# First stage of an LRU-convolution plus LoRA MLP kernel: weight loads, tap tables, the first tile's x and its A product in another order

## The reference, cut to what matters

```python
# x: (64, 32, 512) = batch, head, length
x = x + conv(x, itok_B_8_3872, ...)      # part one, per head h:
#   K[h, l] = 2 Re sum_n Cs[h, n] exp(dtA[h, n] l)      (taps, 64 complex modes)
#   y = causal convolution of x * mask with K[h] + D[h] * x, times mask
x = x + mlp(x, ..., itok_B_2_6, 0)       # part two, per batch row b with its LoRA index:
#   gate = x Wg^T + (x Ag^T) Bg^T / 2 ;  up = x Wu^T + (x Au^T) Bu^T / 2
#   act = silu(gate) * up                (1376 columns)
#   down = act Wd^T + (act Ad^T) Bd^T / 2
```

## Time and profile before

| what | value |
|---|---|
| median of three runs | 562.81 us (562.47 to 563.48) |
| the profiled execution's own time | 563.44 us |
| its span in the trace | 561.6 us |
| granted TensorE clock, mean of the span | 0.993 |
| TensorE busy | 520.0 us, 93% of the span |
| VectorE, ScalarE, GpSimd busy | 46%, 36%, 7% |
| chain of work that ended last | TensorE 86%, VectorE 5%, DMA 5%, SP queue 2% |

### The profile page before, as it was taken

How to read it: one execution, slowest core, us unless ns; L and a number is a source line. 1 busy time by engine, 2 the same in 40 slices (tenths; PEclk the granted TensorE clock), 3 DMA queues, 4 the chain that set the end, 5 groups by cost and what they waited for, 6 DMA issues and landing times.

```text
span 561.6 us, 10112 instructions
## 1 busy us (share of the span) xinstructions
PE 520.0 (93%) x3169; PEld 474.1 (84%) x3169; DVE 258.5 (46%) x556; ACT 199.8 (36%) x426; POOL 39.9 (7%) x55
## 2 busy tenths in 40 slices
PE   0087899999999999999999999999999999999997
PEld 0086787889899998989898989898989898999986
DVE  7855265844343535353535353444444443525341
ACT  4863006534333423232423332333334333324321
POOL 1006600100000000000000000000000000000000
PEclk9998899999999999999999999999999999999999
DMA  7898993304040403040303121121304040404000
GB/s 281 326 299 294 309 350 81 88 6 118 1 118 6 112 11 110 13 110 13 100 22 91 32 81 42 55 68 32 91 13 109 0 123 0 116 7 110 13 20 19
DMA packets 32306, 53.19 MB, mean 95 GB/s; under 512 B 7586, under 2 KB 16194, under 8 KB 32290
## 3 DMA queue, kind: packets, MB, share of 16 engines
q1 hardware_dynamic: 32290, 53.00, 31.7%
HBM read 48.69 MB, written 4.28 MB: 94 GB/s over the span
## 4 chain that ended last, share of the span: by engine, by line
PE 86%; DVE 5%; DMA 5%; SPq 2%; issue 1%; ACT 1%; DVEq 0%
PE ps_u L940 21%; PE ps_g L940 21%; PE ps_db L978 13%; PE ps_da L978 13%; PE ps_x L969 3%; DMA kpad<-k_sb 3%; PE ps_g L892 2%; PE ps_x L919 2%; DMA toep<-kpad 2%; PE ps_u L892 2%; PE ps_g L950 2%; PE ps_g L951 2%; PE ps_u L950 2%; PE ps_u L951 2%; PE ps_x L1011 1%; DVE wd_lo L729 1%
## 5 line engine op out<-in xcount | busy, mean ns | idle before, releaser
L469 ACT CAST b_spl<-b_raw 64x512 fp32r<-64x512 f32 (+1 forms) x96 | 54.5, 571 | 97.1 <-PE ps_u L951 79.1
L766 DVE TENSOR_TENSOR b_spl<-b_raw,b_spl 64x512 fp32r<-64x512 f32 (+1 forms) x96 | 60.7, 633 | 57.0 <-ACT b_spl L469 53.3
L940 PE MATMUL ps_g<-w_hi,x_hi 128*128 128x512 f32 (+1 forms) x192 | 72.7, 379 | 0.2 <-DVE x_lo L759 0.2
L940 PE MATMUL ps_u<-w_hi,x_hi 128*128 128x512 f32 (+1 forms) x192 | 71.3, 371 | 0.0
L940 PE MATMUL ps_u<-w_lo,x_hi 128*128 128x512 f32 (+1 forms) x192 | 71.3, 371 | 0.0
L940 PE MATMUL ps_u<-w_hi,x_lo 128*128 128x512 f32 (+1 forms) x192 | 71.3, 371 | 0.0
L940 PE MATMUL ps_g<-w_lo,x_hi 128*128 128x512 f32 (+1 forms) x192 | 71.1, 370 | 0.0
L940 PE MATMUL ps_g<-w_hi,x_lo 128*128 128x512 f32 (+1 forms) x192 | 71.0, 370 | 0.0
L978 PE MATMUL ps_da<-wd_hi,ht_hi 128*128 128x288 f32 (+1 forms) x176 | 54.6, 310 | 1.4 <-DVE wd_lo L729 1.4
L802 DVE TENSOR_TENSOR h_act<-h_act,ps_u 128x512 f32<-128x512 f32 (+1 forms) x48 | 30.4, 633 | 54.1 <-PE ps_u L951 54.0
L978 PE MATMUL ps_db<-wd_hi,ht_hi 128*128 128x288 f32 (+1 forms) x176 | 53.3, 303 | 0.0
(11 more groups left out here) (165 smaller groups left out, 920.8 us busy)
## 6 DMA issues: line engine op xcount, KB each, us to landing
a_raw<-atab SPq DMA_DIRECT2D x64, 152.0 KB, 2.5
toep<-kpad SPq DMA_DIRECT2D x16, 512.0 KB, 6.3
b_raw<-btab SPq DMA_DIRECT2D x128, 64.0 KB, 2.1
um<-xr SPq DMA_DIRECT2D x16, 256.0 KB, 4.4
x<-xT SPq DMA_DIRECT2D x8, 512.0 KB, 8.4
w_raw<-wgu SPq DMA_DIRECT2D x8, 512.0 KB, 9.1
out<-y_sb SPq DMA_DIRECT2D x15, 256.0 KB, 2.1
b_raw<-btab SPq DMA_DIRECT2D x64, 44.0 KB, 1.8
```

The source lines that it names most:

```text
L469: nc.scalar.copy(b_spl[0:LR, up, 0:w], b_raw[slot][:, up * w:(up + 1) * w]).then_inc(b_hi, 1)
L766: V.tensor_tensor(b_spl[LR:P, up, 0:w], b_raw[slot][:, up * w:(up + 1) * w], b_spl[0:LR, up, 0:w].bitcast(F32), ALU.subtract).then_inc(b_l ...
L940: T.matmul(ps[:, 0:w], xs[:, q, kb, :], ws[:, kb, col:col + w], start=(kb == 0 and xs is x_hi and ws is w_hi), stop=False)
```

## The change

On the SP queue, weight pieces 8 and 9 leave their place ahead of the first store of taps; all of pieces 8 to 11 stand behind Toeplitz loads 0 to 3. The first half of x of group 2 no longer stands ahead of the store of group 1: the four half-groups of x of groups 2 and 3 follow one by one behind the Toeplitz loads of pairs 4 to 7. The stores of group 2 and 3 stand behind the Toeplitz loads of pairs 6 and 7 instead of behind those of pairs 7 and 8. On VectorE `phases(3)` comes before `taps(1)`; `add_conv(0)` ahead of `tables(2)`, and `tables(3)` ahead of `taps(2)`; TensorE does `taps(2)` after conv 2 and `taps(3)` after conv 3.

For the first tile, x is split in two steps: the high and low parts of heads 0 to 27 are made while convs 14 and 15 run; pair 15's result is written first for the four batch rows of the tile, then x of heads 28 to 31 is copied, then the rest of the result is written, and the small high and low parts follow. TensorE's `lora_a(0)` stands behind `base(0, 0)`. In the first tile ScalarE's splits of the down weights start ahead of `silu(0)`, each two pieces one step earlier than before, and VectorE's `rem_part`s likewise.

```diff
@@ SP queue
-            load_piece(2 * KB)
-            load_piece(2 * KB + 1)
             sp.wait_ge(idx_in, 16)
             ids0 = indices(0, 0)
             sp.wait_ge(zero_out, 16)
             store_taps(0)
             for pair in range(RC):
-                load_toep(pair, pair, 0, True)
-            load_piece(2 * KB + 2)
-            load_piece(2 * KB + 3)
-            load_x(2, 0)
+                load_toep(pair, pair, 0)
+            for n in range(2 * KB, NP_GU):
+                load_piece(n)
             store_taps(1)
-            load_x(2, 1)
             for pair in range(RC, 2 * RC):
                 load_um(pair, pair - RC, False)
-                load_toep(pair, pair - RC, 1, False)
-                if pair < RC + 2:
-                    load_x(3, pair - RC)
-            store_taps(2)
+                load_toep(pair, pair - RC, 1)
+                if pair >= RC + 2:
+                    store_taps(pair - RC)
+                load_x(2 + (pair - RC) // 2, pair % 2)
...
                 if pair == 2 * RC:
-                    store_taps(3)
                     load_a(0, 0, ids0)
@@ ScalarE, first tile
+                if first:
+                    top_part(NP_GU)
+                    top_part(NP_GU + 1)
                 silu(0)
                 b_hi_part(a, q, 1, 0)
                 b_hi_part(a, q, 1, 1)
                 if first:
-                    top_part(NP_GU)
-                    top_part(NP_GU + 1)
+                    top_part(NP_GU + 2)
+                    top_part(NP_GU + 3)
...
-            x_hi_part(0, 0, True)
+            act.wait_ge(xt_ok, 1)
+            nc.scalar.copy(x_hi[:, 0, :, 0:(NH - 4) * BT], xt[:, :, 0:(NH - 4) * BT]).then_inc(x0_hi, 1)
+            act.wait_ge(xt_ok, 2)
+            nc.scalar.copy(x_hi[:, 0, :, (NH - 4) * BT:P], xt[:, :, (NH - 4) * BT:P]).then_inc(xhi_ok, 1)
@@ VectorE
+            def select_conv(pair, b0, b1):
+                dve.wait_ge(conv_ps, pair + 1)
+                dve.wait_ge(x_in[2 * pair // HG], 32)
+                return V.copy_predicated(
+                    x[:, 2 * pair:2 * pair + 2, :, b0:b1],
+                    lmask[:, :, b0:b1].unsqueeze(1).broadcast_to([P, 2, KB, b1 - b0]),
+                    ps_c[pair % RC][:, :].rearrange("p (h k b) -> p h k b", h=2, k=KB)[:, :, :, b0:b1])
...
             tables(1)
+            phases(3)
             taps(1)
-            phases(3)
-            tables(2)
-            taps(2)
...
             add_conv(0)
+            tables(2)
             tables(3)
+            taps(2)
+            add_conv(1)
             taps(3)
-            for pair in range(1, PAIRS - 2):
+            for pair in range(2, PAIRS - 2):
...
             take_x(0, NH - 4).then_inc(xt_ok, 1)
             add_conv(PAIRS - 2)
-            add_conv(PAIRS - 1)
-            dve.wait_ge(x1_ok, PAIRS)
+            dve.wait_ge(x0_hi, 1)
+            first_x_lo(0, NH - 4).then_inc(x0_lo, 1)
+            select_conv(PAIRS - 1, 0, BT).then_inc(x0_sel, 1)
+            dve.wait_ge(x1_ok, PAIRS - 1)
+            dve.wait_ge(x0_sel, 1)
             take_x(NH - 4, NH).then_inc(xt_ok, 1)
-            x_lo_part(0, 0, True)
+            select_conv(PAIRS - 1, BT, NB).then_inc(x1_ok, 1)
+            dve.wait_ge(xhi_ok, 1)
+            first_x_lo(NH - 4, NH).then_inc(xlo_ok, 1)
@@ TensorE
             conv(1)
             conv(2)
+            taps(2)
             conv(3)
-            taps(2)
-            conv(4)
             taps(3)
...
-                if first:
-                    lora_a(t)
...
                 if first:
+                    lora_a(t)
                     base(0, 1)
                     lora(0, 0)
```

More of the change, by code:

```diff
@@ L163, in program @@
         conv_ps, x1_ok = sem("conv_ps"), sem("x1_ok")
+        x0_hi, x0_lo, x0_sel = sem("x0_hi"), sem("x0_lo"), sem("x0_sel")
         a_in = sem("a_in")
@@ L217, in program, with taps_rows, shifted_taps @@
         DT, NAR, DAR, DAI = 8, 9, 10, 11
+        def taps_rows(g):
+            return bass.AP(tensor=kpad, offset=g * HG * (P + NL) + P, ap=[[PB, PA], [P + NL, HG], [1, PB]])
+        def shifted_taps(pair):
+            return bass.AP(tensor=kpad, offset=pair * (2 * (P + NL)) + 1, ap=[[1, P], [P + NL, 2], [1, NL]])
         block = top.enter_context(nc.Block())
@@ L235, in store_taps, with load_toep @@
                 sp.wait_ge(k_ready, g + 1)
-                dst = bass.AP(tensor=kpad, offset=g * HG * (P + NL) + P, ap=[[PB, PA], [P + NL, HG], [1, PB]])
-                sp.dma_start(dst, k_sb[:, g, :, :]).then_inc(k_out[g], 16)
-            def load_toep(pair, slot, group, first):
+                sp.dma_start(taps_rows(g), k_sb[:, g, :, :]).then_inc(k_out[g], 16)
+            def load_toep(pair, slot, group):
                 sp.wait_ge(k_out[group], 16)
[L242 to L245, removed]
+                wait(sp, conv_ps, pair - RC + 1)
+                sp.dma_start(toep[:, slot, :, :], shifted_taps(pair)).then_inc(toep_in[slot], 16)
             def load_um(pair, slot, first):
@@ L317, in _ @@
                 load_um(pair, pair % RC, False)
-                load_toep(pair, pair % RC, pair // RC, False)
+                load_toep(pair, pair % RC, pair // RC)
                 if pair == 2 * RC:
-                    store_taps(3)
                     load_a(0, 0, ids0)
@@ L525, in body @@
                 if first:
-                    top_part(NP_GU + 2)
-                    top_part(NP_GU + 3)
-                ht_hi_part(0)
-                if first:
                     top_part(NP_GU + 4)
                     top_part(NP_GU + 5)
+                ht_hi_part(0)
                 silu(2)
@@ L819, in body @@
                 V.tensor_tensor(cols(wd_lo), ad, cols(wd_hi).bitcast(F32), ALU.subtract).then_inc(ad_lo, 1)
+                if first:
+                    rem_part(NP_GU)
+                    rem_part(NP_GU + 1)
                 b_lo_part(a, q, 1, 0)
@@ L828, in body @@
                 if first:
-                    rem_part(NP_GU)
-                    rem_part(NP_GU + 1)
+                    rem_part(NP_GU + 2)
+                    rem_part(NP_GU + 3)
                 b_lo_part(a, q, 2, 0)
@@ L834, in body @@
                 if first:
[L835 to L838, removed]
                     rem_part(NP_GU + 4)
                     rem_part(NP_GU + 5)
+                ht_lo_part(0)
                 if not last:
@@ L857, in _, with first_x_lo @@
             b_lo_part(0, 0, 0, 1)
+            def first_x_lo(h0, h1):
+                cols = slice(h0 * BT, h1 * BT)
+                return V.tensor_tensor(x_lo[:, 0, :, cols], xt[:, :, cols], x_hi[:, 0, :, cols].bitcast(F32),
+                                       ALU.subtract)
             dve.wait_ge(x1_ok, PAIRS - 2)
@@ L904, in _ @@
             conv(2)
+            taps(2)
             conv(3)
-            taps(2)
-            conv(4)
             taps(3)
-            for pair in range(RC + 1, PAIRS):
+            for pair in range(RC, PAIRS):
                 conv(pair)
@@ L934, in base @@
                     if c == 0 and not up:
+                        if first:
+                            pe.wait_ge(x0_lo, 1)
                         pe.wait_ge(xlo_ok, t + 1)
```

## The result

The changed kernel takes 559.44 us (median of 5 executions, 558.71 to 560.04) against 562.47 us of the kernel before (5 executions, 562.13 to 563.48): a ratio of 0.9943, 95% interval 0.9929 to 0.9957. It is 3.0 us faster where 1.95 were predicted; the span of the profiled execution goes from 561.6 to 557.6 us.

The account below looks back on a forecast made before the run. The first 106 us, a chain of waits through DMA stores, x preparation and tile 0, were taken as the bound. -2.5 - 1.05 + 1.6 = -1.95 us from 562.81 gave 560.8 us; forecast 559.5 to 561.7, range with rivals 558.2 to 563.2.

Parts of the forecast that it names:

- Stretch 1: From the start to the landing of pair 9's Toeplitz matrix: 2.5 us earlier, with ends of 0.4 and 4.
- The main term: Group 2's store no longer empties the DMA queue at 50 to 58 us: 3.4 us gained.
- The gain at the first store: Without pieces 8 and 9 ahead, group 0's store lands at 24.8 instead of 25.73: gain 0.95 (0 to 0.95).
- the first part: Within the first stage: 0.95 us gained at group 0's store, 1.8 lost to pieces 8 and 9 behind Toeplitz loads.
- The order of the tables: VectorE's new order ahead of the taps costs nothing, covered by 4 us or more of queued traffic.
- Stretch 2: From conv 15's end to the first base product: 2.50 us becomes about 1.45, gain 1.05 (0.5 to 1.1).
- Stretch 3: Tile 0, first base product to down product: 20.5 us becomes about 22.05, loss 1.6 (0.9 to 2.5).
- Both waits: TensorE's new waits in tile 0: 1.05 us for the low part of B, about 1.1 at the x transposes.
- The queue gives more: Rival: pieces fill holes, pair 9 lands 4 us earlier, TensorE's lower clock mostly avoided; about 558.5 us, chance 0.17.
- The queue gives nothing: Rival: first reads of a group made the hole, the first stage gains only 0.4 to 0.8; 562.4 us, chance 0.20.
- The clock falls at the start of tile 0: Rival: TensorE idleness before the base group halves 12 base matmuls' rate, costing 1.8; 564.8 or 564.4 us, chance 0.08.
- lengthened by a drain: Rival: a drain at ScalarE's table load in tile 0 adds 1.38 us; 562.2 us, chance 0.03.

Follow-up runs that it names:

- the experiment on it: Old order of tables and taps on VectorE and TensorE put back in the changed kernel, SP queue as changed: 558.35 us, ratio 0.9935 to the kernel before.

## Why the prediction was right, and where its terms were off

**Direction and range.** Right: 559.44 lies in 558.2 to 563.2, on the better side of 560.8. The forecast's own narrower range, 559.5 to 561.7, is missed by 0.06.

**Stretch 1, 2.5 predicted, 3.65 at pair 9's start.** The main term, the hole behind group 2's store, was right in mechanism and place: the landing at 49.36 was put at 49, and with the stores back pair 9 starts 3.66 us later and the median is 4.2 higher, where 3.4 was taken. The step that failed is the one that charged 1.8 us for pieces 8 and 9 "ahead of all that pair 9 needs". It counted bytes as if the queue were full up to pair 9; it was not, it drained around store 1, and most of the bytes fell into that hole. What they cost is the 2.65 - 2.08 = 0.6 us of store 1. I had given the hole as the lower end of that term and took the upper end without a row for it.

The gain at the first store was too small: it landed 1.32 us earlier, outside "0 to 0.95". I had the queue full until 23.7, but it moved only 84 GB/s from 22 to 24 us, and the store took 1.75 us, less than the 2.08 that I had called its floor. Then a chain carries the gain on, Toeplitz load 0, conv 0 (4.95 us where the next ones take 2.62, with a granted clock of 1.00 in its stretch; why is not shown), `taps(1)`, and store 1 is issued 1.47 us earlier; its landing is 0.9 earlier. From there to pair 9's start it is 2.7 us more, where the hole was put at 3.4. So the sum came out within 1.2 us partly by luck, as two errors cancel: the first part was put at -0.85 and gave +0.9, the second was put 0.7 too high.

**The order of the tables.** Costed at nothing, with 4 us of queued traffic as cover: right, as the experiment on it shows. `k_ready` of group 2 came at 42.45, later than the 41 to 42 predicted, as the last small step of the taps took 2.27 us beside GpSimd; the cover hid it.

**Stretch 2.** 1.05 predicted, 1.13 found; the small `copy_predicated` takes 0.19 where 0.20 was taken.

**Stretch 3.** -1.6 predicted, -0.98 found. Both waits are at their places; the mis-sized terms are their lengths, 0.57 for 1.05 and 0.25 for 1.1. ScalarE's `silu(0)` starts 9.6 us behind the base product, as computed; but TensorE itself arrives later at both points, because `lora(0, 0)` waits 0.3 rather than 0.1 us, and VectorE's last two splits take 1.82 rather than 2.2.

**The signs.** The two stores landed where they were put, and the two waits in tile 0 are at their places but shorter. One sign did not come: no stretch between 46 and 60 us was to move under 200 GB/s, and 58 to 60 moved 193. It is no hole, since the DMA engines were busy throughout (share 1.10).

```profile
58.00:60.00 2.00, 0.54 (x5) 0.41 (x4) 0.73 (x1) 0.00 (x0) 2.00 (x2) 1.00 1.10 193
```

**The rivals.** "The queue gives more" (558.5, chance 0.17) came nearer to the result than the forecast, and its first half holds: the pieces fill a hole. Its second does not: the gap ahead of conv 9 is 2.34 us, and conv 9 ran at the lower clock, 4.15 us. "The queue gives nothing" has a slip in its sum: with 0.4 to 0.8 from stretch 1 the terms give 562.6 to 563.0, not 562.4. "The clock falls at the start of tile 0" did not happen, the first 12 base matmuls take 3.04 us behind 1.38 us of idleness, as against 3.03 before. The later `silu(0)` is not lengthened by a drain: 90.44 - 89.14 is the 1.28 of the load and 0.02. By the rule of the Trainium skill (ScalarE: Activation LUTs, What ACT_TABLE_LOAD costs) 1.38 us more were due; the trace disagrees here too.

## What to carry to other kernels

Where a queue is worked in order, put what waits for a computation as early as its data allows, and put bulk traffic behind it that waits for nothing: a 16 KB store at the end of a burst emptied the queue for 3 us. Before bytes are charged to a path, look for a stretch on it in which the queue runs dry: 1.8 us of traffic moved to such a place cost 0.6 us here. An operation that ran in a gap for nothing is not free at its new place, and its follow-up work on other engines starts later too: moving a 0.9 us product cost 2.7 us at the median.

## What the runs showed of the hardware that I had not expected

**The same gap, two clocks.** In the profiles of these kernels, one each, gaps of 2.05, 2.11, 2.17 and 2.66 us ahead of conv 9 were followed by a conv of 2.62 us, gaps of 2.17, 2.34, 2.47 and 2.61 by one of 3.9 to 4.3. The granted clock around conv 9, in the changed kernel and then in the first profile with the A product in front:

```profile
60.00:62.00 2.00, 1.12 (x3) 0.94 (x4) 0.00 (x0) 0.10 (x1) 2.00 (x2) 0.66 1.02 311
62.00:64.00 2.00, 2.00 (x9) 1.91 (x8) 0.00 (x0) 1.03 (x2) 2.00 (x2) 0.50 1.05 387
...
60.00:62.00 2.00, 1.35 (x9) 1.30 (x10) 0.00 (x0) 0.34 (x1) 2.00 (x2) 1.00 1.03 329
```

The length of the gap does not decide between 2.4 and 1.2 GHz here; what does is not shown. It is a part of the spread between executions of one program: the changed kernel's three with a mean granted clock of 0.995 or 0.996 took 559.44 to 560.04 us, the two with 0.998 and 0.999 took 558.90 and 558.71. The Trainium skill (TensorE: Matmul & The Clock Gate, Part 1) says that the number of matmuls at the lower level varies between runs of one kernel; by that the trace agrees. Two profiles, one on each side, can then differ by 1.5 us (4.15 against 2.62 for conv 9) that no edit made, and I took rows of one execution for a rule.

**GpSimd slows VectorE.** A `tensor_tensor` with both inputs in SBUF, 0.88 us alone, takes 1.7 to 2.9 us while GpSimd runs its own; an add of eight elements takes 2.26 us (40.19 in the changed kernel) instead of 0.16. `copy_predicated` from PSUM stays at 0.73 in the same time. The Trainium skill (GPSIMD Engine Reference, Specifications) says that the two share SBUF interfaces, with contention for VectorE instructions that have two SBUF inputs; the trace agrees. GpSimd's own instruction beside them took 2.3 us (40.05 in the changed kernel, four in 9.31) to 2.6 us (65.22 above, four in 10.58).
